# Row statistics of five layer norms taken in the tail of the layer ahead, and two early loads in the delta layer

## What is computed

```python
def _layernorm(x, axis=-1, eps=1e-05):
    m = jnp.mean(x, axis=axis, keepdims=True)
    v = jnp.var(x, axis=axis, keepdims=True)
    return (x - m) / jnp.sqrt(v + eps)

x = x + deltanet(_layernorm(x), ...)        # 0 dn: linear recurrence, 8 heads, own output norm
x = x + sine_ffn(_layernorm(x), ...)        # 1 sf: 128 -> 512, sine transform, relu, -> 128
x = x + test_time_mlp(_layernorm(x), ...)   # 2 tt: an MLP trained step by step, then applied
x = x + dense_experts(_layernorm(x), ...)   # 3 de: gate over 8 experts, thresholded, all of them
x = x + attention(_layernorm(x), ...)       # 4 sa: 8 heads; takes one more norm of its input
x = x + channel_mix(_layernorm(x), ...)     # 5 cm: shifted mix, sigmoid gate, squared relu
x = x + flash_attention(_layernorm(x), ...) # 6 ba: 16 heads of 8, blocks of 64 keys, out_w, out_b
x = x + routed_ffn(_layernorm(x), ...)      # 7 rf: top 2 of 8 experts, and a shared expert
```

## Time and profile before

| | before |
|---|---|
| runs | 2617.99 us median of 3 (2617.76 to 2619.3) |
| profiled execution | 2618.58 us, span 2616.7 us |
| mean granted TensorE clock | 0.865 of full speed |
| TensorE busy | 2051.6 us, 78% |
| VectorE busy | 1846.0 us, 71% |
| ScalarE busy | 1330.3 us, 51% |
| GpSimd busy | 510.7 us, 20% |
| chain that ended last, by engine | PE 47%, DVE 29%, issue 9%, ACT 6%, DMA 3%, SP queue 2%, POOL 2% |

### The profile page before, as it was taken

The page is one execution under the profiler, slowest core; times in us unless marked ns, Lnnn a source line. Parts: engine busy times, 40 slices in busy tenths (PEclk is TensorE's granted clock), DMA queues, the critical chain, the costliest instruction groups (busy, mean ns, idle before and its releaser), DMA issues.

```text
span 2616.7 us, 63828 instructions
## 1 busy us (share of the span) xinstructions
PE 2051.6 (78%) x20012; PEld 1148.7 (44%) x20012; DVE 1846.0 (71%) x3796; ACT 1330.3 (51%) x2738; POOL 510.7 (20%) x936
## 2 busy tenths in 40 slices
PE   4449875688888768559999984659999999999745
PEld 2336553467777543224444433413333333333434
DVE  4856657755655457758888865569999999999571
ACT  3311105533333220327777763538888888888622
POOL 3322332034444210101111110001111111111203
PEclk9755557899999879869999997769999999999877
DMA  2342210000000000131111100221111111111001
GB/s 58 79 116 68 68 48 13 8 0 0 0 0 0 1 9 0 33 93 32 33 34 31 37 13 3 56 75 36 36 36 37 37 37 37 37 37 34 22 0 32
DMA packets 140879, 86.60 MB, mean 33 GB/s; under 512 B 67338, under 2 KB 120211, under 8 KB 140756
## 3 DMA queue, kind: packets, MB, share of 16 engines
q1 hardware_dynamic: 140756, 84.95, 12.3%
HBM read 57.01 MB, written 27.26 MB: 32 GB/s over the span
## 4 chain that ended last, share of the span: by engine, by line
PE 47%; DVE 29%; issue 9%; ACT 6%; DMA 3%; SPq 2%; POOL 2%; DVEq 1%; POOLq 0%; ACTq 0%; PEldq 0%
PE psum L2131 9%; DVE ba_blockmax L2341 8%; PE psum L2109 8%; PE psum L2120 6%; DVE X L1296 2%; PE psum L2140 2%; PE psum L659 2%; DVE dn_arena L939 1%; ACT tt_sg L1649 1%; DVE tt_aT L1704 1%; PE psum L648 1%; DMA ba_qs<-ba_mparts 1%; PE psum L1611 1%; PE psum L682 1%; PE psum L1620 1%
## 5 line engine op out<-in xcount | busy, mean ns | idle before, releaser
L2341 DVE TENSOR_REDUCE ba_blockmax<-psum 128x16 f32<-128x1024 f32 x512 | 607.5, 1215 | 58.0 <-PE psum L2109 37.5
L2213 ACT ACTIVATE ba_pt<-psum 128x512 f32<-128x512 f32 x1024 | 554.2, 597 | 104.3 <-PE psum L2120 87.9
L2109 PE MATMUL psum<-ba_ks,ba_qs 64*128 64x512 bf16 x1024 | 343.7, 416 | 65.3 <-DMA ba_qs<-ba_mparts 22.1
L2343 DVE TENSOR_REDUCE sa_negmax<-psum 128x1 f32<-128x1024 f32 x256 | 304.4, 1221 | 85.6 <-PE psum L2109 77.8
L2213 ACT ACTIVATE sa_pt<-psum 128x512 f32<-128x512 f32 x512 | 269.9, 599 | 116.1 <-PE psum L2120 113.3
L2131 PE MATMUL psum<-ba_pt,ba_vh 128*32 128x256 f32 x4096 | 314.5, 390 | 0.1
L2120 PE MATMUL psum<-ba_qs,ba_ks 64*128 64x512 bf16 x1024 | 313.6, 380 | 0.8 <-DMA ba_qs<-ba_mparts 0.4
L2109 PEld LDWEIGHTS psum<-ba_ks,ba_qs 64*128 64x128 bf16 x1024 | 116.8, 148 | 256.9 <-issue 254.3
L2109 PE MATMUL psum<-sa_ks,sa_qs 96*128 96x512 bf16 x512 | 207.2, 410 | 27.7 <-DMA sa_ks<-sa_kstk 24.4
L2120 PE MATMUL psum<-sa_qs,sa_ks 128*128 128x512 bf16 x512 | 194.4, 383 | 1.5 <-ACT sa_pt L2213 1.5
L2131 PEld LDWEIGHTS psum<-ba_pt,ba_vh 128*32 128x32 f32 x4096 | 92.3, 108 | 154.5 <-issue 146.5
(11 more groups left out here) (475 smaller groups left out, 3860.7 us busy)
## 6 DMA issues: line engine op xcount, KB each, us to landing
ba_qs<-ba_qstk SPq DMA_DIRECT2D x128, 48.0 KB
ba_ks<-ba_kstk SPq DMA_DIRECT2D x128, 48.0 KB
dn_pst<-dn_arena SPq DMA_DIRECT2D x32, 128.0 KB, 2.5
dn_tst<-dn_arena SPq DMA_DIRECT2D x8, 512.0 KB, 5.8
dn_arena<-dn_tst SPq DMA_DIRECT2D x8, 512.0 KB, 4.1
dn_arena<-dn_pst SPq DMA_DIRECT2D x8, 512.0 KB, 5.4
ba_qs<-ba_qstk SPq DMA_DIRECT2D x128, 32.0 KB
ba_ks<-ba_kstk SPq DMA_DIRECT2D x128, 32.0 KB
```

Of the source, the lines that this page charges most:

```text
L2109: last = nc.tensor.matmul(bank(2 * slot + h), qs[b][0:KP, :].rearrange("p (a r) -> p r a", r=NTB)[:, r, :], ks[b][0:KP, h * HALF:(h + 1) * ...
L2213: nc.scalar.activation(pt[x_][:, :, h * P:(h + 1) * P].rearrange("p j (a m) -> p j a m", m=2), bank(4 + slot).rearrange("p (a j m) -> p j ...
L2341: ins = nc.vector.tensor_reduce(blockmax[g][:, r, :], src.rearrange("p (n s) -> p n s", s=BLOCK), AXX, ALU.max, negate=True)
L2343: ins = nc.vector.tensor_reduce(negmax[g][:, r:r + 1], src, AXX, ALU.max, negate=True)
```

## The change

A class `Early` holds a division of the 32 tiles into pieces. While a layer runs its tail, VectorE takes statistics, aggregates and the addition of EPS for each piece as soon as its tiles of X are final, GpSimd raises each piece's variances to -1/2 (`roots`), and the next `layer_norm` starts with `shift`. Statistics, means, variances and roots live in buffers of their own that outlast a layer. The last piece is taken behind `layer_done`.

- dn: eight pieces of four tiles (every eighth); pieces 0 to 3 in slots of the recurrence's turns, 4 to 7 at its end.
- tt and `project_out`: eight pieces of four tiles, piece g - 1 ahead of the addition of group g.
- cm: four pieces of eight tiles, after the next batch's `mix`; the VectorE loop is unrolled.
- sa: pieces of 16, 14 and 2 tiles, the first two ahead of the last head's work.
- `weights` runs in the second attention's norm after the fourth of eight groups, in the first's between the two powers. `clear` is cut into four parts, which ScalarE runs after its passes 0 to 3 of the projections; SP and GpSimd wait for `cleared` 4, TensorE for `ready` 1. ScalarE's projection loop is unrolled.
- dn: `load(0)` and `load(1)` are issued at the head of step 6 of 8 (m == M - 2), each behind a wait for its own stores of `pst`.

The norms at the head of dn, tt and sa (behind nothing, sf and de) take their statistics as before; those of sf, de, cm, ba and rf are the five that the title speaks of.

```diff
+        self.stats = self.sb("row_stats", [P, NT, 6])
+        self.mv = self.sb("row_mv", [P, NT, 2])
+        self.var = self.sb("row_var", [P, NT])
+        self.rstd = self.sb("row_rstd", [P, NT])
+        self.varied = self.sem("varied")
+        self.rooted = self.sem("rooted")
+        self.pieces = 0
+        self.early = None
...
+class Early:
+
+
+    def __init__(self, k, tag, pieces):
+        self.k, self.pieces, self.first = k, pieces, k.pieces
+        self.own, self.n = k.sem(f"{tag}_early_own"), 0
+        k.pieces += len(pieces)
+        k.early = self
+
+    def place(self, x, j):
+
+        first, step, count = self.pieces[j]
+        return x[:, first:first + step * (count - 1) + 1:step]
+
+    def tiles(self, j):
+        first, step, count = self.pieces[j]
+        return [first + step * n for n in range(count)]
+
+    def stats(self, v, tiles):
+        for n in tiles:
+            self.k.nc.vector.bn_stats(self.k.stats[:, n, :], self.k.X[:, n, :]).then_inc(self.own, 1)
+            self.n += 1
+
+    def aggregate(self, v, tiles):
+        v.wait_ge(self.own, self.n)
+        for n in tiles:
+            self.k.nc.vector.bn_aggr(self.k.mv[:, n, :], self.k.stats[:, n, :]).then_inc(self.own, 1)
+            self.n += 1
+
+    def spread(self, v, j):
+        v.wait_ge(self.own, self.n)
+        self.k.nc.vector.tensor_scalar(self.place(self.k.var, j), self.place(self.k.mv[:, :, 1], j), EPS, None,
+                                       ALU.add).then_inc(self.k.varied, 1)
+
+    def whole(self, v, j):
+        self.stats(v, self.tiles(j))
+        self.aggregate(v, self.tiles(j))
+        self.spread(v, j)
+
+    def roots(self, p, j):
+        p.wait_ge(self.k.varied, self.first + j + 1)
+        self.k.nc.gpsimd.tensor_tensor(self.place(self.k.rstd, j), self.place(self.k.var, j), self.k.mhalf[:, 0:self.pieces[j][2]],
+                                       ALU.pow).then_inc(self.k.rooted, 1)
+
+    def rooted_for(self, tiles):
+        return self.first + 1 + max(j for j in range(len(self.pieces)) if set(self.tiles(j)) & set(tiles))
...
+    early, k.early = k.early, None
     ready = [k.sem(f"{tag}_ready{g}") for g in range(2)]
     ready_a = [k.sem(f"{tag}_ready_a{g}") for g in range(2)]
     shift_in = k.sem(f"{tag}_shift_in")
     turned = [k.free_sem(f"{tag}_turned{g}") for g in range(2)]
     written = [k.free_sem(f"{tag}_xt{g}") for g in range(2)]
-    var_in, root_out = k.sem(f"{tag}_var"), k.sem(f"{tag}_root")
-    own = k.sem(f"{tag}_ln_own")
     ctx = k.layer_ctx
     xn = [k.sb(f"{tag}_xn{g}", [P, GROUP, D], ctx=ctx) for g in range(2)]
-    stats = k.sb(f"{tag}_st", [P, NT, 6], ctx=ctx)
-    mv = k.sb(f"{tag}_mv", [P, NT, 2], ctx=ctx)
-    root = k.sb(f"{tag}_root_buf", [P, NT], ctx=ctx)
-    rstd = k.sb(f"{tag}_rs", [P, NT], ctx=ctx)
-    tmp = k.sb(f"{tag}_ln_tmp", [P, 2, NT], ctx=ctx)
+    stats, mv, rstd = k.stats, k.mv, k.rstd
...
+            if early and second_vector is not None:
+                second_vector(v)
...
-                v.wait_ge(root_out, (3 if twice else 1) + h)
+                if early:
+                    v.wait_ge(k.rooted, early.rooted_for(range(halves[h].start, halves[h].stop)))
+                if twice or not early:
+                    v.wait_ge(root_out, (1 if early or not twice else 3) + h)
...
+            if early and not twice and g == NG // 2 and second_vector is not None:
+                second_vector(v)
...
-        if first_scalar is not None:
-            first_scalar(a)
...
-        for q in range(2 if twice else 1):
+        for q in range(1 if early else 0, 2 if twice else 1):
...
+    early = Early(k, "dn", [(m, M, B) for m in range(M)])
...
+        def load(m):
+            s.wait_ge(t_stored[m // 2], 32)
+            s.wait_ge(p_stored[m % 2], stores(m))
+            if m >= 2:
+                s.wait_ge(xa_out, Q * (m - 1))
+                s.wait_ge(pv_done, Q * (m - 1))
+            s.dma_start(macro(Tt[m % 2]), of_macro(tst, m)).then_inc(t_loaded[m % 2], 16)
+            s.dma_start(macro(Pm[m % 2]), of_macro(pst, m)).then_inc(p_loaded[m % 2], 16)
+
         for m in range(M):
+            if m == M - 2:
+                load(0)
+                load(1)
...
-        for z in range(2):
-            s.wait_ge(p_stored[z], stores(M - 2 + z))
-
-        def load(m):
-            s.wait_ge(t_stored[m // 2], 32)
-            if m >= 2:
-                s.wait_ge(xa_out, Q * (m - 1))
-                s.wait_ge(pv_done, Q * (m - 1))
-            s.dma_start(macro(Tt[m % 2]), of_macro(tst, m)).then_inc(t_loaded[m % 2], 16)
-            s.dma_start(macro(Pm[m % 2]), of_macro(pst, m)).then_inc(p_loaded[m % 2], 16)
-
-        load(0)
-        load(1)
...
+            if m >= 5:
+                early.roots(p, m - 5)
+        for m in range(M - 5, M - 2):
+            early.roots(p, m)
         add(M - 1)
+        early.roots(p, M - 2)
         p.wait_ge(x_in, M)
         p.sem_inc(k.layer_done, 1)
+        early.roots(p, M - 1)
...
+                if c >= 3 * Q + 3 and c % Q == 3 and c < NCH - 1:
+                    m = c // Q - 3
+                    if y == 0:
+                        v.wait_ge(x_in, m + 1)
+                    early.stats(v, early.tiles(m)[y * B // 2:(y + 1) * B // 2])
+                if c >= 4 * Q and c % Q == 0:
+                    m = c // Q - 4
+                    if y == 0:
+                        early.aggregate(v, early.tiles(m))
+                    else:
+                        early.spread(v, m)
         measure(M - 1)
         normalise(M - 1)
+        for m in range(M - 4, M):
+            v.wait_ge(x_in, m + 1)
+            early.whole(v, m)
...
+    early = Early(k, "cm", [(b * 2 * GROUP, 1, 2 * GROUP) for b in range(B)])
...
-        with v.Fori(0, B) as i:
+        for i in range(B):
             for g in range(2):
                 mix(i, g)
+            if i:
+                early.whole(v, i - 1)
             for g in range(2):
                 add(i, g)
             c.restart()
         nc.vector.tensor_copy(part[0][:, 0:1], part[0][:, 0:1]).then_inc(k.layer_done, 1)
+        early.whole(v, B - 1)
...
+    def gpsimd(p):
+        for b in range(B):
+            early.roots(p, b)
...
+    early = Early(k, "tt", [(g * GROUP, 1, GROUP) for g in range(NG)])
...
+            if g:
+                v.wait_ge(added[1 - z], (g - 1) // 2 + 1)
+                early.whole(v, g - 1)
...
+        early.whole(v, NG - 1)
...
-    def clear(a):
+    def clear(a, piece):
+
         c_ = Chain(a, a_own)
 
         def fill(tile, value):
             c_.do(nc.scalar.activation(tile, k.mhalf[0:tile.shape[0], 0:1].to_broadcast(list(tile.shape)), ACT.Identity, scale=-2.0 * value))
 
-        for g in range(3):
-            fill(qs[g][:, :], 0.0)
-            fill(ks[g][:, :], 1.0)
-            fill(vh[g][:, :, :].rearrange("p n e -> p (n e)"), 0.0)
-        fill(vall[:, :, :, :].rearrange("p n t e -> p (n t) e")[:, :, HD], 0.0 if blocked else 1.0)
-        c_.sync()
-        if blocked:
-            fill(vall[P - BLOCK:P, :, NTB - 1, HD], 1.0)
+        if piece < 3:
+            fill(qs[piece][:, :], 0.0)
+            fill(ks[piece][:, :], 1.0)
+            fill(vh[piece][:, :, :].rearrange("p n e -> p (n e)"), 0.0)
+        else:
+            fill(vall[:, :, :, :].rearrange("p n t e -> p (n t) e")[:, :, HD], 0.0 if blocked else 1.0)
+            c_.sync()
+            if blocked:
+                fill(vall[P - BLOCK:P, :, NTB - 1, HD], 1.0)
         c_.restart()
-        a.sem_inc(ready, 1)
+        a.sem_inc(cleared, 1)
...
-        s.wait_ge(ready, 2)
+        s.wait_ge(cleared, 4)
...
-        with a.Fori(0, B) as i:
+        for i in range(B):
...
+                if 2 * i + g < 4:
+                    clear(a, 2 * i + g)
...
+        early = Early(k, tag, [(0, 1, N // 2), (N // 2, 1, N // 2 - 2), (N - 2, 1, 2)])
...
+        if not blocked:
+            early.roots(p, 0)
+            early.roots(p, 1)
         add(Head(0, N - 1))
         if not blocked:
             p.wait_ge(added, N + 1)
             p.sem_inc(k.layer_done, 1)
+            early.roots(p, 2)
...
+                if not blocked and c == N - 1 and x_ == 0:
+                    v.wait_ge(added, N - 1)
+                    early.whole(v, 0)
+                    early.whole(v, 1)
...
+            v.wait_ge(added, N + 1)
+            early.whole(v, 2)
...
+    early = Early(k, tag, [(g * GROUP, 1, GROUP) for g in range(NG)])
...
+                if b or g:
+                    v.wait_ge(added[1 - g], b + g)
+                    early.whole(v, 2 * b + g - 1)
...
+        early.whole(v, NG - 1)
...
+        for g in range(NG):
+            early.roots(p, g)
```

63 lines of the change are left out of this document (37 added, 26 removed).

## The result

The changed kernel takes 2595.52 us (median of four runs, 2595.17 to 2599.97) against 2617.97 before: ratio 0.991, 95% interval [0.9898, 0.9921]. It is 22.45 us faster; 18.7 were forecast, 2599.3 us in the range of 2591 to 2610.

The account below looks back on a forecast made before the run. Bound: the chain of waits, 47% TensorE and 29% VectorE, mostly in the untouched attentions, so only seams and tails count. Terms -9.9-3.0-3.3-7.0-1.5-3.3+1.4+2.4+5.5 sum to -18.7 us: 2599.3 us, range 2591 to 2610.

Parts of the forecast that it names:

- TensorE then waits only for `p_in`: Delta layer: with early loads TensorE starts the recurrence at about 163.2 instead of 173.15, -9.9 us.
- Rival 2: Delta layer: early loads pay almost nothing, only 2 of 9.9 us are left; 2607 us in all; 8%.
- Slots in the recurrence: 0.: Delta layer: statistics in the recurrence hide in VectorE's 0.78 us idleness, cost 0; without the cover 5.9 us.
- The weights are last.: Seams between layers: readers come sooner and loads later, so weight loads, with 6 to 11 us slack before, limit the gain.
- Rival 1: Seams: weights are not last, each gains what its norm does, from -7.9 to +1.3 us; 2585 us in all; 8%.
- the loads later, since `arrived` now follows the last piece's statistics and power: Seams: `arrived` comes 2.8 us later behind a last piece of four tiles, delaying the next layer's weight loads.
- The fills: Both attentions' projections: fills moved there delay the second buffer's ScalarE step, +1.4 us in the first, +2.4 in the second.
- Rival 3: Attention projections: every piece of the fills stands on the path, +17.1 us instead of 3.8; 2612.6 us in all; 7%.
- The sign of the last seam.: Seam into routed_ffn: the tail ends 8.6 us later, loads slip 11.4, TensorE waits for them: +5.5 us (+1.3 to +7).
- The seam into dense_experts.: Seam behind tt: `shift` comes 5.8 us sooner, but the weights land at 946.3 against the old reader's 949.65: -3.3 us.
- Powers do not hold VectorE.: Tails: GpSimd additions hold VectorE up and powers don't, so the new powers cost the tails nothing.
- Rival 4: Tails, recurrence and norms: GpSimd powers lock VectorE out, +22.8 us; 2622 us in all, slower; 4%.

Follow-up runs that it names:

- experiment 1: The changed kernel again, no edit: 2595.89 us, ratio 0.9902; its profiled execution took 2593.52 us.
- experiment 5: The kernel before with only `load(0)` and `load(1)` issued early, at the head of step 6: 2610.89 us against 2621.22, ratio 0.9963.
- experiment 6: The kernel before with only channel_mix's VectorE loop unrolled: 2622.49 us against 2621.22, ratio 1.0007.
- the first trace: The first profiled execution of the changed kernel, no edit: 2599.97 us.
- experiment 7: The changed kernel with the delta layer's pieces 0 to 3 taken behind the recurrence instead of in its slots: 2597.49 us.
- experiment 2: The changed kernel with each layer's weight loads issued ahead of the wait for `arrived` and the clears: 2580.67 us, ratio 0.9833.
- experiment 12: The kernel of experiment 2 with ScalarE writing the fills of pieces 0 to 2 of both attentions twice: 2595.9 us.
- experiment 3: The changed kernel without pieces in `project_out`, so the last norm takes its own statistics: 2593.03 us.
- experiment 4: The changed kernel with weight loads ahead of the turnover and no pieces in `project_out`: 2582.73 us.
- experiment 9: The changed kernel with both attentions' fills as GpSimd memsets issued once `layer_done` is up, instead of ScalarE's in the projections: 2599.64 us.

## Why the prediction was right, and where it was off

**The sum was partly luck.** The mechanisms were right, and the terms less exact than the total. In experiment 1's trace the parts with a forecast other than 0 add up to about -30 us, 11 more than the 18.7 of the sum. The parts that were put at 0 (recurrence, rest of sine_ffn, heads, rest of routed_ffn) gave 5.5 of it back, and not all of that belongs to the change (experiments 5 and 6 have the recurrence's excess without it). Against the kernel before as timed beside experiment 1 (2623.22), the same changed kernel gains 27.3 us, as much as the far end of the range allows.

**The chain through the loads.** The sentence "TensorE then waits only for `p_in`" held: 162.70 for a forecast 163.2, and experiment 5 shows -10.3 for this edit alone. Rival 2 is out. The slower load of `L` was in the bounds and cost nothing.

**Slots in the recurrence: 0.** Right, although the first trace seemed to show +2.7. Experiments 5, 6 and 7 show an excess of 0.9 to 2.0 without them, and it varies as much with them.

**The weights are last.** This was the step that made the forecast 18.7 and not 33. Experiment 2 shows it directly: with the loads out of the way the same pieces give 11.75 to 15.2 us more, and the releasers go back to those of before. Rival 1 (2585) described what happens if the weights are not last; experiment 2 is that kernel, with 2580.67 beside a before of 2623.22. It gains 42.6 us by the medians and 36.8 by the traces, where rival 1 had 33.

**Mis-sized terms.** At three of the four seams with a gain the forecast was 1 to 2 us short (-3.0, -7.0, -3.3 for -4.6, -8.0, -5.0). The term "the loads later, since `arrived` now follows the last piece's statistics and power", taken at its full 2.8 us in sine_ffn and 4.6 in the second attention, was too large. In sine_ffn, from GpSimd's last addition of X to the first weight load it was 6.5 us and is 8.0 (386.21 to 394.21): 1.5 later, not 2.8. The other seams agree, and the figure is the same in both traces of the changed kernel: from the end of the layer's work to the first weight load it is 1.6 more into dense_experts and 1.3 more into routed_ffn where 2.8 was taken, 0.9 where 1.9 was (channel_mix), and 2.3 where 4.6 was (second attention). This is the term that was mis-sized most often. The old 6.5 already held some microseconds of SP's clears and waits, which a later `arrived` partly overlaps; how they overlap I did not measure. In the last tail, "8.6 later" was priced at 2.4 us a group, the length of a lone piece and addition; the measured group is 2.12 and the slip 6.6. The fills cost 0.3 to 1.1 and 0.8 to 1.2 us, where 1.4 and 2.4 were taken: what cover they found in the cycle was not measured, only that it is used up (experiment 12). Rival 3, with 17.1, is out. The loop of channel_mix gave 2.0 to 2.8 for a forecast 1.5.

**The sign of the last seam.** Forecast +5.5, seen +2.8 and +3.3 against before and +1.7 against experiment 3; experiments 3 and 4 show that the late loads, and not the pieces as such, are the reason.

**The seam into dense_experts.** -3.3 forecast, -3.0 in experiment 1, +1.6 in the first trace. That -3.0 meets the forecast because two misses cancel. The forecast let `layer_done` slip by 1.5 and the loads by 2.8 more; the slips were 0.4 and 1.6, so the reader came 5.0 us sooner after the first addition than before (34.67 for 39.72). Behind the wait for the weights (3.45 us) TensorE then did its second group of eight products onwards at half clock, 1.71 us each, where before the first three groups took 0.9 to 1.0 each; that took 1.7 back. In the first trace there was one more group at the lower clock in the tail, SP took 1.36 us to issue the load of `de_gb` (0.43 in experiment 1), and behind a stall of 4.44 us all products ran at half clock.

**Powers do not hold VectorE.** Rival 4 is out. In the last tail a power runs beside each addition and each set of statistics, and the period is the sum of VectorE's own steps, 2.12 us, with the addition at the same 0.69 as before. A form nearer to the rule of the Trainium skill (SBUF — State Buffer, "Who interferes with whom") is VectorE's normalising step from SBUF to SBUF. Each of the four steps that start beside the power of 1.02 us at 2447.57 takes 0.34 us (they overlap, so that six of them fit into 1.62 us), as do the steps beside no GpSimd work, while a memset holds such a step until it ends (experiment 9). The measurement agrees with the rule for GpSimd's additions. For memsets it agrees with the Trainium skill's clause (same section) on VectorE's two-port modes, which asks of GpSimd no read of SBUF, if this step runs in such a mode; no run shows that. It does not agree for GpSimd's powers.

**Left open.** The heads of the second attention and the rest of routed_ffn are each 2.1 to 2.5 us longer in both executions of the changed kernel. In the heads, experiment 6, which changes nothing there, shows the same +2.3, and experiment 5 about 0, so it need not be the change. In routed_ffn, from the first weight reader to the end, both executions of the changed kernel take 137.7 us, before 135.4, experiments 5 and 6 134.4 and 134.2, and the other kernels with the change 135.1 to 136.7. What it is was not found in either place.

## What to carry over

When work moves out of the head of a stage, ask what else was hidden behind that head. Here it was the weight loads of the stage, issued behind a turnover that waits for all engines: a good part of what the norms lost came back as a wait for them (up to 5.4 us at a seam), and one edit had the wrong sign until the loads were issued earlier. The pieces in the delta layer, channel_mix and the first attention were not taken out one by one; what they are worth is known from the shifts alone. Where one execution is several microseconds above the next, judge a small edit by its own stage, in two executions at least, and by a kernel that has that edit alone.

## What the hardware showed unexpectedly

- TensorE's granted clock at one place of the same code was 0.50 in one execution and 0.94 in another, worth 2.9 us in a tail of 22; at the last attention head it fell early in one execution of experiment 6, worth about 7.
- GpSimd's memset, which reads nothing, held VectorE's SBUF to SBUF steps until it ended (0.80 to 1.05 us instead of 0.34), while GpSimd powers of 1.0 and 3.0 us did not lengthen them.
- In the recurrence, TensorE pauses of about 0.3 to 1 us for which the profile names no releaser come and go between executions, up to 2.8 us in all beyond those of the profiled execution of before; the one at chunk 13 was there in eight of fourteen executions, and in just these a DMA packet of instructions had started 6.1 to 6.5 us after the one before it instead of 3.8 to 4.0.
